# Pairing the value and expert matmuls of a fused attention and mixture-of-experts kernel, and computing values and gates as one float32 product

## The reference, cut to what matters

```python
xn = layernorm(x)                                   # x: (32, 256, 128)
q, k, v = xn @ Wq.T + bq, xn @ Wk.T + bk, xn @ Wv.T + bv      # 16 heads of 8
attn = softmax(causal(q @ k.T / sqrt(8))) @ v       # per head
att = attn @ Wo.T + bo
top_val, top_idx = top_k(xn @ gate_w.T, 2)          # 8 experts
ffn = sum over the two of softmax(top_val) * (xn @ We[top_idx])
out = x + att + ffn
```

## Time and profile before

| | |
|---|---|
| median of 3 runs | 563.18 us (563.01 to 564.31) |
| the profiled execution's own time | 564.58 us |
| its span, first to last instruction | 562.8 us |
| mean granted clock of PE | 0.993 of full speed |

### The profile page before, as it was taken

The page is one execution under the profiler, slowest core; times in us unless marked ns, Lnnn a source line. Parts: engine busy times, 40 slices in busy tenths (PEclk is TensorE's granted clock), DMA queues, the critical chain, the costliest instruction groups (busy, mean ns, idle before and its releaser), DMA issues.

```text
span 562.8 us, 19500 instructions
## 1 busy us (share of the span) xinstructions
PE 516.0 (92%) x6402; PEld 402.3 (71%) x6402; DVE 439.1 (78%) x1109; ACT 400.9 (71%) x1033; POOL 346.4 (62%) x565
## 2 busy tenths in 40 slices
PE   1157999999999999999999999999999999999986
PEld 1145777777777777777777787777777778777754
DVE  3268888888888888888888888888888888877721
ACT  5624677777777777778777777777877777776664
POOL 4323576666666777666666677766666667754433
PEclk9999999999999999999999999999999999999988
DMA  3645555464455555544544555554445455540000
GB/s 98 172 98 139 137 138 137 110 145 125 110 132 137 145 137 135 134 130 120 128 128 117 137 145 136 131 139 126 128 118 133 115 139 147 137 130 12 12 12 20
DMA packets 64002, 67.11 MB, mean 119 GB/s; under 512 B 6752, under 2 KB 59104, under 8 KB 59104
## 3 DMA queue, kind: packets, MB, share of 16 engines
q1 hardware_dynamic: 63968, 66.68, 47.0%
HBM read 44.90 MB, written 21.23 MB: 118 GB/s over the span
## 4 chain that ended last, share of the span: by engine, by line
PE 79%; ACT 7%; DMA 4%; issue 4%; DVE 3%; POOL 2%; SPq 1%; ACTq 1%; POOLq 0%; DVEq 0%
PE m L779 26%; PE oT_ps L847 14%; PE scoreT_ps L823 10%; PE score_ps L803 9%; PE scoreT_ps L828 6%; PE score_ps L797 4%; ACT probs L473 3%; PE m L956 3%; DMA qstack<-mT 2%; PE m L951 2%; ACT parts L496 2%; PE m L893 1%; PE m L925 1%; DMA x_sb<-in_x 1%; PE m L914 1%
## 5 line engine op out<-in xcount | busy, mean ns | idle before, releaser
L589 DVE TENSOR_REDUCE negmax<-score_ps 128x2 f32<-128x512 f32 (+1 forms) x384 | 260.4, 686 | 51.9 <-PE score_ps L803 37.8
L473 ACT ACTIVATE probs<-scoreT_ps 128x512 f32<-128x512 f32 x384 | 225.8, 607 | 88.7 <-PE scoreT_ps L823 44.5
L779 PE MATMUL m<-we_hl,xnT_hl 128*128 128x512 f32 x384 | 122.9, 429 | 0.0
L847 PE MATMUL oT_ps<-probs,vaug 128*32 128x256 f32 (+1 forms) x2048 | 110.2, 333 | 0.0
L823 PE MATMUL scoreT_ps<-qstack,kstack 123*128 123x128 bf16 (+1 forms) x1024 | 102.7, 222 | 5.1 <-DMA qstack<-mT 4.5
L803 PE MATMUL score_ps<-kstack,qstack 72*128 72x128 bf16 (+1 forms) x1024 | 104.3, 224 | 1.9 <-DVE negmax L589 1.8
L372 POOL TENSOR_TENSOR fours<-lower,upper 128x512 f32<-128x512 f32 x64 | 81.8, 1278 | 22.1 <-ACT upper L508 21.3
L823 PEld LDWEIGHTS scoreT_ps<-qstack,kstack 123*128 123x128 bf16 (+1 forms) x1024 | 68.3, 98 | 33.1 <-issue 21.6
L366 POOL TENSOR_TENSOR parts<-rest,parts 128x256 bf16<-128x256 f32 x64 | 41.9, 673 | 72.0 <-ACT parts L501 71.6
L847 PEld LDWEIGHTS oT_ps<-probs,vaug 128*32 128x32 f32 x2048 | 53.6, 109 | 37.6 <-issue 5.4
L803 PEld LDWEIGHTS score_ps<-kstack,qstack 72*128 72x128 bf16 (+1 forms) x1024 | 71.1, 100 | 5.6 <-DVE negmax L589 3.8
(11 more groups left out here) (82 smaller groups left out, 696.6 us busy)
## 6 DMA issues: line engine op xcount, KB each, us to landing
kstack<-scratch SPq DMA_DIRECT2D x96, 192.0 KB
scratch<-parts SPq DMA_DIRECT2D x64, 192.0 KB, 2.4
qstack<-scratch SPq DMA_DIRECT2D x64, 192.0 KB
qstack<-scratch SPq DMA_DIRECT2D x32, 256.0 KB
x_sb<-in_x SPq DMA_DIRECT2D x32, 128.0 KB, 2.1
scratch<-parts SPq DMA_DIRECT2D x32, 128.0 KB, 1.9
out<-out_sb SPq DMA_DIRECT2D x32, 128.0 KB, 1.9
qstack<-mT SPq DMA_DIRECT2D x64, 8.0 KB, 1.8
```

Source lines behind the costliest of these rows:

```text
L473: a.activation(o, i, ACT.Exp, scale=SCALE).then_inc(act_exp, 1)
L589: v.tensor_reduce(o, score_ps[n % 2][:].rearrange("p (h k) -> p h k", h=w), axis=AX.X, op=ALU.max, negate=True).then_inc(dve_max, 1)
L779: ins = tn.matmul(o, l, r, start=i == 0, stop=i == len(products) - 1)
L847: ins = tn.matmul(o, va[:, q, h, :], i, start=q == 0 and grp % VGRP == 0, stop=q == 1 and grp % VGRP == VGRP - 1, skip_group_check=True)
```

## The change

`values` runs for two groups in a row: groups 2 and 3 at step 5, groups 0 and 1 at step 10, each after the transposed item of the step; `probs` gets four buffers instead of two. The expert items run in pairs, at steps 3 and 8, ahead of the transposed item. Values and gates become one float32 product per half of the tokens, from a float32 copy `xnT` of the transposed input that ACT makes at step 11; DVE's split of the input now waits for that copy. The transposes of the input move from step 11 to step 10, ahead of the others there. ACT copies `oT` after its exponential of step 6 instead of step 5, and scales expert tiles at steps 4 and 9 instead of 6 and 11; DVE scales its first at step 4 instead of 5. The preparation of the split value weights goes.

```diff
@@ -136,7 +136,6 @@
         wvg_sb = sb("wvg_sb", [P, VG])
-        wvg_hl = sb("wvg_hl", [P, 2, VG], FP32R)
         wo_sb = sb("wo_sb", [P, D])
@@ -153,6 +152,7 @@
         xb = sbs("xb", [P, QT, D])
+        xnT = sbs("xnT", [P, S])
         xnT_hl = sbs("xnT_hl", [P, 2, S], FP32R)
@@ -160,7 +160,7 @@
         weight = sbs("weight", [P, QT, E])
-        probs = sbs("probs", [P, 3, HG, P], n=2)
+        probs = sbs("probs", [P, 3, HG, P], n=NG)
@@ -169,7 +169,6 @@
         w_high = sb("w_high", [P, E, D])
-        wvg_high = sb("wvg_high", [P, VG])
         parts = sb("parts", [P, 2, PARTS, S], BF16)
@@ -218,7 +217,7 @@
         dve_stats, dve_mv, pool_eps, pool_rstd, pool_xn = sems("dve_stats", "dve_mv", "pool_eps", "pool_rstd", "pool_xn")
-        pe_xnT, dve_halves, act_high, pool_xb = sems("pe_xnT", "dve_halves", "act_high", "pool_xb")
+        pe_xnT, act_xnT, dve_halves, act_high, pool_xb = sems("pe_xnT", "act_xnT", "dve_halves", "act_high", "pool_xb")
         pe_qk, act_part1, dve_rest, act_part2, pool_part3 = sems("pe_qk", "act_part1", "dve_rest", "act_part2", "pool_part3")
@@ -397,7 +396,7 @@
                 for n in range(ITEMS):
-                    if n == (1 if has(s, -1) else 3) and has(s, -2):
+                    if n == 0 and has(s, -2):
                         sum_tile(t + (-2), 1)
@@ -444,7 +443,7 @@
                                         bias_out[:].unsqueeze(1).to_broadcast([P, QT, D]), ALU.add).then_inc(pool_xb, 1)
-                    if n == 10 and has(s, -1):
+                    if n == 9 and has(s, -1):
                         sum_tile(t + (-1), 0)
@@ -456,14 +455,10 @@
                 grp, j = k // 3, k % 3
-                pr = probs[grp % 2]
+                pr = probs[grp]
                 act.wait_ge(pe_scoreT, upto(f, per=ITEMS, k=k + 1))
                 if j == 0:
-
-                    if grp >= 2:
-                        act.wait_ge(pe_pv, upto(f, per=NG, k=grp - 1))
-                    else:
-                        act.wait_ge(pe_pv, upto(f + (-1), per=NG, k=NG + grp - 1))
+                    act.wait_ge(pe_pv, upto(f + (-1), per=NG, k=grp + 1))
                 if j < 2:
@@ -525,14 +520,16 @@
                         take_values(t, s)
-                    if n == 11 and has(s, -1):
-                        upper_experts(t + (-1), 1)
+                    if n == 11 and has(s, NXT):
+                        nxt = t + NXT
+                        act.wait_ge(pe_xnT, upto(nxt))
+                        a.copy(xnT[nxt.buf][:], m1[:, 0:S]).then_inc(act_xnT, 1)
                     f, k = behind(t, s, n)
...
                         part2(t + PRE, n - 2)
-                    if n == 5 and has(s, -2):
+                    if n == 6 and has(s, -2):
                         fin = t + (-2)
@@ -546,8 +543,8 @@
                         a.copy(oTn[:], m0[:, 0:S]).then_inc(act_oTn, 1)
-                    if n == 6 and has(s, -1):
-                        upper_experts(t + (-1), 0)
+                    if n in (4, 9) and has(s, -1):
+                        upper_experts(t + (-1), 0 if n == 4 else 1)
@@ -561,8 +558,6 @@
                     act.wait_ge(dve_weights, 3)
-                    a.copy(wvg_hl[:, 0], wvg_high[:]).then_inc(act_weights, 1)
-                    act.wait_ge(dve_weights, 5)
                     a.copy(we_hl[:, 0], w_high[:]).then_inc(act_weights, 1)
@@ -648,7 +643,7 @@
                 if k == 0:
-                    dve.wait_ge(pe_xnT, upto(nxt))
+                    dve.wait_ge(act_xnT, upto(nxt))
                     dve.wait_ge(act_high, upto(nxt + (-1)))
@@ -677,7 +672,7 @@
                         total(t)
-                    if n == 5 and has(s, -1):
+                    if n == 4 and has(s, -1):
                         lower_experts(t + (-1), 0)
@@ -745,9 +740,6 @@
                     dve.wait_ge(ld_w, 16 * NW)
-                    high_half(wvg_sb[:], wvg_high[:]).then_inc(dve_weights, 1)
-                    dve.wait_ge(dve_weights, 3)
-                    low_half(wvg_sb[:], wvg_high[:], wvg_hl[:, 1]).then_inc(dve_weights, 1)
                     dve.wait_ge(dve_zero, 1)
@@ -760,7 +752,7 @@
                     high_half(we_sb[:], w_high[:]).then_inc(dve_weights, 1)
-                    dve.wait_ge(dve_weights, 5)
+                    dve.wait_ge(dve_weights, 3)
                     low_half(we_sb[:], w_high[:], we_hl[:, 1]).then_inc(dve_weights, 1)
@@ -771,12 +763,11 @@
-            def by_halves(o, high, low, other_high, other_low, whole=False):
-
-
-                products = [(high, other_high), (high, other_low), (low, other_high)] + [(low, other_low)] * whole
-                for i, (l, r) in enumerate(products):
-                    ins = tn.matmul(o, l, r, start=i == 0, stop=i == len(products) - 1)
+            def by_halves(o, high, low, other_high, other_low):
+
+
+                for first, l, r in ((True, high, other_high), (False, high, other_low), (False, low, other_high)):
+                    ins = tn.matmul(o, l, r, start=first, stop=l is low)
                 return ins
@@ -836,7 +827,7 @@
                     pe.wait_ge(act_oT, upto(f + (-1)))
-                pr, va = probs[grp % 2], vaug[f.buf]
+                pr, va = probs[grp], vaug[f.buf]
                 c0 = S * (grp // VGRP)
@@ -867,8 +858,8 @@
                 if s == 1 and d == 0:
-                    pe.wait_ge(dve_weights, 6)
-                    pe.wait_ge(act_weights, 3)
+                    pe.wait_ge(dve_weights, 4)
+                    pe.wait_ge(act_weights, 2)
                 cols = slice(q * P, (q + 1) * P)
@@ -882,7 +873,7 @@
                         scoreT_item(f, k)
-                    if n == 11 and has(s, NXT):
+                    if n == 10 and has(s, NXT):
                         pe.wait_ge(pool_xn, upto(t + NXT))
@@ -898,12 +889,9 @@
                             pe.wait_ge(dve_lower, upto(fin, per=2))
-                        if s == 0:
-                            pe.wait_ge(dve_weights, 4)
-                            pe.wait_ge(act_weights, 2)
                         for q in range(QT):
-                            ins = by_halves(m1[:, q * VG:(q + 1) * VG], xnT_hl[t.buf][:, 0, q * P:(q + 1) * P],
-                                            xnT_hl[t.buf][:, 1, q * P:(q + 1) * P], wvg_hl[:, 0], wvg_hl[:, 1], whole=True)
+                            ins = tn.matmul(m1[:, q * VG:(q + 1) * VG], xnT[t.buf][:, q * P:(q + 1) * P], wvg_sb[:],
+                                            start=True, stop=True)
                         ins.then_inc(pe_vg, 1)
@@ -913,12 +901,10 @@
                         ins.then_inc(pe_mT, 1)
-                    if n == 3 and has(s, -2):
-                        values(fin, NG - 2)
-                    if n in (9, 11) and has(s, -1):
-                        values(mix, (n - 9) // 2)
                     if n in EXPERT_STEPS and has(s, -1):
-                        experts(mix, s, EXPERT_STEPS.index(n))
+                        q = EXPERT_STEPS.index(n)
+                        experts(mix, s, 2 * q)
+                        experts(mix, s, 2 * q + 1)
                     if n == 10 and has(s, -2):
@@ -927,7 +913,11 @@
                     if n == 5 and has(s, -2):
-                        values(fin, NG - 1)
+                        values(fin, 2)
+                        values(fin, 3)
+                    if n == 10 and has(s, -1):
+                        values(mix, 0)
+                        values(mix, 1)
                     if n == 1 and has(s, PRE):
@@ -962,7 +952,7 @@
-            EXPERT_STEPS = (4, 6, 8, 10)
+            EXPERT_STEPS = (3, 8)
             pe.wait_ge(pool_const, CONSTS + 2)
```

## The result

The changed kernel takes 664.71 us (median of 4 runs, 663.39 to 664.85) against 563.1: a ratio of 1.179, 95% interval 1.177 to 1.182. Slower was forecast, at 649 us in a range of 618 to 690. The profiled execution has a span of 661.6 us, where the prediction's sum gave 648.8.

A forecast was written before the change was run, and what follows sets the result against it. PE's matmul stream was taken to set the 15.63 us slot. Five new waits, 4.17 a slot, less 1.03 saved, gave 119.6 less 32 over the run, 2 off for early slots: 649 us, range 618 to 690.

The forecast's parts named there:

- The savings: On PE per slot: float32 values and gates 0.41, value pairs 0.26, expert pairs 0.20, one stall 0.16; sum 1.03 us.
- The value pair: Two value groups in a row on PE: second costs 0.75 without change-over, saving 0.13 us a pair, 0.26 in all.
- The expert pair: Second expert item on PE has weights loaded behind a matmul: 0.69 instead of 0.79, saving 0.10 us a pair.
- The stall of 0.16: Transposed item after step 3's value group, held by ACT's exponential behind the bias step, stops waiting; saves 0.16 us.
- The five waits: PE waits: second expert item 0.86, step 5 transposed item 0.15, oT transposes 0.86, input transposes 1.40, values and gates 0.90.
- the 0.16 of step 5: PE's transposed item at step 5 waits for the exponential of the item two before; forecast 0.15 us.
- The waits don't replace one another.: After each PE wait come long items and the next producer starts behind it, so all five add: 4.17 us a slot.
- ACT gets a copy ... and has room: ACT's added 128x256 copy takes under 0.59 us a slot; ACT, busy 71%, has room for it.
- PE staying the bound: Rival: producers keep pace, PE stays the bound and only the savings show, 531 us; chance 5%.
- Half of the waits: Rival: maxima and exponentials follow faster or ACT copies oT sooner; waits 2, 3 and another go, 594 us; 12%.
- The clock: Rival: PE's idle time lowers its granted clock, adding about 3 us a slot, or 735 us; chance 10%.
- the float32 product gives nothing: Rival: float32 values and gates save nothing on PE, slot grows by 0.41, 662 us; no separate chance given.

The follow-up runs named there:

- e7: Changed kernel with one value pair and one expert pair kept, items re-placed to cover producers, keys filled first, fewer ACT waits: 554.64 us, 0.987 of the kernel before.
- e12: Kernel before with its hardware loop written out: 560.83 us, ratio 0.999 to the kernel before.
- e1: Changed kernel with ACT's oT copy back at step 5: 669.94 us.
- e2: Changed kernel with the input transposes back in step 11, behind the value pair: 645.9 us.
- e4: Changed kernel with the first expert pair split, item 0 at step 3 and item 1 at step 6: 660.71 us.
- e3: Changed kernel with the pair of value groups 0 and 1 in step 11 behind score item 11, instead of step 10: 644.43 us.
- e5: Changed kernel with ACT filling the constant key rows before its waiting copy of the transposed input in the first slots: 663.26 us.
- e6: Changed kernel with the hardware loop written out, same instructions: 651.39 us.
- e10: Changed kernel without ACT's wait for pe_pv before each group's first exponential, 258 ACT instructions in the loop: 659.28 us.
- e8: Kernel before with only the float32 values-and-gates product and ACT's copy of the transposed input, at step 10: 581.37 us.

## Why the prediction was right

- **What bounds the kernel.** Right: PE's stream before, no engine after. PE's share fell to 77% (about 80% forecast).
- **The savings.** Values and gates cost 0.57 behind the wait, and 0.52 where they don't wait, as in e7; I took 0.53. The value pair costs 1.44 with 0.10 to change over, 1.54 instead of 1.76: saved 0.22 a pair, where I took 0.13; the same 32 instructions last 1.51 here and lasted 1.61 in the row that I went by the earlier trace rows. The expert pair costs 315.38 - 313.89 = 1.49, saved 0.09 (0.10). The stall of 0.16 is gone; e12 shows its size. Together (0.37, 0.44, 0.18, 0.16) 1.15 instead of 1.03, for the pairs that don't wait inside. The four passes for true FP32 of the Trainium skill's page "FP8 and Floating Point Precision", section TensorE Precision Notes, read as a time, would have given nothing for the first term; the rows of both forms, 0.94 and 0.52 to 0.57, decide against that reading.
- **The five waits.** All are there, at the places named; sum 4.28 against 4.17. The view names the forecast releaser for the four large ones; for the 0.16 of step 5 it names none, and the end of the exponential, 0.06 before PE's item, is what fits. The one that was short by 0.12 is the input transposes: 0.10 of it is their handover, which took 0.15, not 0.05. With the savings of 1.15 the sum gives a slot of 18.75; 0.11 of the measured 18.86 is not placed.
- **"The waits don't replace one another."** Right for adding them up, which is what the forecast needed. It doesn't hold for taking one away: e1 gave 0.44 of 0.86, e2 0.84 of 1.52, e4 0.21 of 0.86; only e3 gave all. Behind the wait that ends last stands the next chain, which POOL, `o_sb` or a DMA ends.
- **The start.** The step that fell short is "ACT gets a copy ... and has room". ACT had the room (in the middle of the trace its copy ends at 319.93, and DVE's maximum ahead of the split at 321.18), but in the first slots the copy waits for PE and 3.6 us of key filling stand behind it. The prediction asked what queues behind each waiting instruction of PE and didn't ask it of ACT's. 4.4 us, of which e5 takes away 3.9.
- **The loop's edge.** No step of the prediction looked at it. 4.7 us, shown by e6 and e10. With the start it makes 9.1 us of a miss of 12.8 in the span; that the time still lay inside 618 to 690 is owed to bounds that were set for other terms, the savings and the waits.
- **The rivals.** PE staying the bound: its saving is real (e8's slot, e7's time) but it needed another order. Half of the waits: refuted, all five are there. The clock: 0.999 in the changed kernel, and 0.963 in e1 with one wait fewer. That the float32 product gives nothing is refuted by e8's slot.

## What to carry to other kernels

When the busiest engine issues in order, an item's place is worth more than its length. For each data item that it needs, measure from the instruction that starts the producer chain to the end of the last producer, and compare with the work that it issues in between; grouping long items takes that cover from what stood between them, and it helps only what the pair still stands in front of (e3 moved a pair behind the start of a chain and got its whole wait back). Before crediting a wait's removal, look for the chain that ends second. And a copy added to an engine with time to spare still has a place in its stream and a share in its loop body: its 0.4 us a slot cost nothing here, its place cost 4.4 us at the start and its share in the loop 4.7.

## What the runs showed of the hardware that I had not expected

- ACT stood 2.1 us (up to 4.1 in e2) at the jump of a hardware loop with 273 instructions of its own in the loop, and not at all with 269 or 258; the packets of its instruction queue went from 15 to 40. In a kernel where PE is full (e8) that made 2.5 to 5.3 us an edge.
- The granted clock of PE fell to 0.50 behind an idle piece of 1.64 us in about half of the slots of e1, and fell at three of the five edges of e8 (2.34 us idle at one of them, while one that kept the clock had 2.00); in the changed kernel, with 1.35 us once and 0.6 to 0.7 three times a slot, it stayed at 1.00. Other slots of e1 with the same order kept it too, so the idle piece alone doesn't decide.
- Written out, the loop's ordinary slot is 0.33 us shorter where the chain of the query product is bare (18.86 against 18.53), and 0.16 to 0.17 in the kernel before (15.62 against 15.45). That waits against register values instead of constants are the cause is likely but not isolated.
